# Flow attention: inverses as 128 columns, spread by plain fp32 matmuls one chunk at a time

## What is computed

```
q = sigmoid(q); k = sigmoid(k)
sink_incoming    = 1 / sum_d((q + EPS) * (k.sum(n) + EPS))
source_outgoing  = 1 / sum_d((k + EPS) * (q.sum(n) + EPS))
conserved_sink   = sum_d((q + EPS) * ((k * source_outgoing).sum(n) + EPS)) + EPS
conserved_source = clip(sum_d((k + EPS) * ((q * sink_incoming).sum(n) + EPS)) + EPS, -1, 1)
v    = v * softmax_n(conserved_source) * n
kv   = k^T v                                     # 32 x 32 in each head
out  = (q * sink_incoming) kv * sigmoid(conserved_sink)
out  = out @ proj_w.T + proj_b
```

## Time and profile before

| | |
|---|---|
| time, median of 3 runs | 2605.04 us (2602.89 to 2608.36) |
| profiled execution: its own time | 2608.17 us |
| its span on the core | 2606.3 us |
| mean granted clock of TensorE | 0.979 |
| TensorE busy | 2350.9 us, 90% of the span |
| VectorE busy | 1591.2 us, 61% |
| ScalarE busy | 1247.5 us, 48% |
| GpSimd busy | 691.7 us, 27% |

### The profile page before, as it was taken

One profiled execution on the slowest core, in us unless ns is written; L12 is line 12 of the kernel. 1 busy time (PEld: TensorE's weight loads), 2 busy tenths in 40 slices (PEclk: granted clock), 3 DMA queues, 4 the chain that ended last, 5 costly groups with the idle time before them and its releaser, 6 DMA issues.

```text
span 2606.3 us, 37060 instructions
## 1 busy us (share of the span) xinstructions
PE 2350.9 (90%) x13000; PEld 1303.8 (50%) x13000; DVE 1591.2 (61%) x3101; ACT 1247.5 (48%) x2870; POOL 691.7 (27%) x989
## 2 busy tenths in 40 slices
PE   7989999989988999998898999999899899999866
PEld 3655544545565544454556554435455655444443
DVE  4664643569866462457977655155797746516698
ACT  5763212259675321227967431222886723122396
POOL 0002140037401232013820213201480031310366
PEclk9999999999999999999999999999999999999988
DMA  8001010010210200001030101001003010100000
GB/s 300 18 11 49 24 45 33 0 49 1 87 50 10 72 29 17 32 1 49 9 128 2 55 26 29 32 17 49 1 9 128 2 58 23 29 17 1 0 1 33
DMA packets 58988, 99.43 MB, mean 38 GB/s; under 512 B 13364, under 2 KB 13748, under 8 KB 58296
## 3 DMA queue, kind: packets, MB, share of 16 engines
q1 hardware_dynamic: 58808, 97.06, 11.3%
HBM read 88.66 MB, written 8.39 MB: 37 GB/s over the span
## 4 chain that ended last, share of the span: by engine, by line
PE 61%; DVE 18%; ACT 14%; issue 4%; POOL 2%; DMA 0%; ACTq 0%; DVEq 0%; POOLq 0%; SPq 0%
PE psum L398 20%; PE psum L392 13%; ACT prob L810 6%; PE psum L424 4%; PE psum L483 3%; DVE neg_max L1106 3%; PE psum L549 2%; DVE f_a L1113 2%; PE psum L451 2%; PE psum L791 2%; DVE bn L1056 2%; DVE f_top L1392 2%; PE psum L620 1%; ACT f_z L1008 1%; PE psum L763 1%
## 5 line engine op out<-in xcount | busy, mean ns | idle before, releaser
L398 PE MATMUL psum<-weights,mixed 128*128 128x512 f32 x768 | 341.2, 595 | 0.0
L392 PE MATMUL psum<-xT,weights 128*128 128x512 f32 x768 | 334.5, 593 | 0.0
L810 ACT ACTIVATE prob<-psum,neg_max 128x128 f32<-128x128 f32 (+3 forms) x512 | 265.0, 543 | 109.3 <-DVE neg_max L1106 109.3
L1430 POOL TENSOR_SCALAR var<-stats 128x1 f32<-128x1 f32 x192 | 63.8, 332 | 797.2 <-DVE stats L1057 797.1
L1106 DVE TENSOR_REDUCE neg_max<-psum 128x1 f32<-128x128 f32 (+3 forms) x512 | 217.5, 483 | 81.2 <-PE psum L488 46.5
L846 ACT COPY xT<-psum 128x512 f32<-128x512 f32 x128 | 70.3, 590 | 367.4 <-PE psum L451 367.4
L1087 DVE TENSOR_TENSOR x<-psum,x 128x512 f32<-128x512 f32 x128 | 88.4, 691 | 244.8 <-PE psum L398 172.7
L398 PE MATMUL psum<-weights,xT 128*128 128x512 f32 x512 | 232.9, 598 | 2.4 <-DVE recip L1295 1.6
L1443 POOL TENSOR_TENSOR f_a<-f_a,f_z 128x256 f32<-128x256 f32 x256 | 204.5, 809 | 113.8 <-DVE f_a L1113 113.8
L392 PEld LDWEIGHTS psum<-xT,weights 128*128 128x128 f32 x768 | 144.0, 190 | 172.4 <-issue 172.2
L398 PEld LDWEIGHTS psum<-weights,mixed 128*128 128x128 f32 x768 | 141.6, 190 | 167.5 <-issue 166.7
(11 more groups left out here) (246 smaller groups left out, 4193.1 us busy)
## 6 DMA issues: line engine op xcount, KB each, us to landing
xT<-in_xT SPq DMA_DIRECT2D x8, 1024.0 KB, 6.4
x<-in_x SPq DMA_DIRECT2D x8, 1024.0 KB, 8.9
out<-x SPq DMA_DIRECT2D x16, 512.0 KB, 2.8
weights<-in_a_k SPq DMA_DIRECT2D x4, 1024.0 KB, 5.3
weights<-in_a_q SPq DMA_DIRECT2D x4, 1024.0 KB, 5.1
weights<-in_a_v SPq DMA_DIRECT2D x4, 1024.0 KB, 5.0
w1f<-in_w SPq DMA_DIRECT2D x4, 1024.0 KB, 14.9
w2f<-in_w SPq DMA_DIRECT2D x4, 1024.0 KB, 17.3
```

The lines of the kernel that those rows point to most:

```text
L392: last = mm(bank[:, 0:n], weights[weight][:, c, heads(g)], rhs(c), start=(c == 0), stop=(c == C - 1))
L398: last = mm(bank, lhsT(c), weights[weight][:, c, :], start=(c == 0), stop=(stop and c == C - 1))
L810: last = run(sb["prob"][:, slot, o:o + keys], bank[:, o:o + keys], ACT.Exp, bias=sb["neg_max"][:, n, qc, j:j + 1], accum_out=sb["a_sum"][: ...
```

## The change

The inverses are held as 128 columns instead of 512: a quarter (tile) c of a window is laid on partitions 2c and 2c + 1 of each head's eight. For that a total is computed by 16 matmuls of 128 columns (`d_quarters`: four quarters of four chunks, accumulated) with `d_thin` widened to four quarters. The split in coarse half and remainder is gone from ScalarE and GpSimd; each spread bank is filled by four plain fp32 matmuls of 32 rows (those of the chunk), 128 stationary columns (`d_sel`) and 128 moving columns (`d_inv`), chunk after chunk. The two source sums go to one bank (256 columns), with one exponential and one transpose of 128x128 for each window. Each of the four constants has its own `d_weights` and `d_sums`; the one for the q sums, a total and a spread move in among the last projections of k. `d_project` is a step for each chunk. In this stage `dve_ring` has banks 6 and 7 as well. The core of the diff (left out: declarations of tiles, semaphores and constants, and the same steps in other words):

```diff
+    def widen(self, banks):
+
+        n = len(self.names)
+        k = (n - self.first) % len(self.banks)
+        self.banks, self.first = banks + self.banks[k:] + self.banks[:k], n
+
+    def narrow(self, pe, banks):
+
+        self.drained(pe)
+        self.banks = banks
...
-              ("weight", 12), ("transpose", 3, 4), ("d_project", 0, 0), ("transpose", 3, 5), ("transpose", 3, 6), ("transpose", 3, 7),
-              ("d_project", 0, 1), ("bias", 3, 0), ("bias", 3, 1), ("d_project", 1, 0), ("d_project", 1, 1)]
+              ("weight", 12), ("transpose", 3, 4)]
+    steps += [("d_project", 0, 0, g) for g in range(C)] + [("transpose", 3, 5), ("transpose", 3, 6), ("transpose", 3, 7)]
+    steps += [("d_project", 0, 1, g) for g in range(C)] + [("bias", 3, 0), ("bias", 3, 1)] + [("d_project", 1, 0, g) for g in range(C)]
+    steps += [("d_weights", OF_Q), ("d_project", 1, 1, 0), ("d_sums", OF_Q), ("d_total", 1), ("d_project", 1, 1, 1), ("d_project", 1, 1, 2),
+              ("d_spread", 1), ("d_project", 1, 1, 3), ("d_table",)]
     if b < B - 1:
         steps += [("weight_ahead", 1), ("weight_ahead", 2)]
-    steps += [("d_sums",), ("d_total", 0), ("d_turn", 0), ("d_total", 1), ("d_turn", 1), ("d_value", 0), ("d_turn", 2), ("d_value", 1),
-              ("d_spread", 0), ("d_total", 2), ("d_value", 2), ("d_turn", 3), ("d_spread", 1), ("d_total", 3), ("d_value", 3), ("d_turn", 4),
-              ("d_value", 4), ("d_spread", 2), ("d_value", 5), ("d_turn", 5), ("d_value", 6), ("d_spread", 3), ("d_value", 7), ("d_turn", 6),
-              ("d_turn", 7), ("d_sums2",), ("d_source", 0), ("d_source", 1), ("d_sink", 0, 0), ("d_sink", 0, 1), ("d_weigh", 0), ("d_weigh", 1), ("d_sink", 0, 2), ("d_sink", 0, 3), ("d_kv",)]
+    steps += [("d_turn", 0), ("d_turn", 1), ("d_total", 3), ("d_weights", OF_K), ("d_value", 0), ("d_sums", OF_K), ("d_total", 0), ("d_spread", 3),
+              ("d_value", 1), ("d_total", 2), ("d_spread", 0), ("d_weights", OF_SINK), ("d_value", 2), ("d_turn", 2), ("d_spread", 2),
+              ("d_value", 3), ("d_sums", OF_SINK), ("d_weights", OF_SOURCE), ("d_value", 4), ("d_turn", 3),
+              ("d_sums", OF_SOURCE), ("d_source",), ("d_value", 5), ("d_turn", 4), ("d_turn", 5), ("d_value", 6), ("d_weigh", 0), ("d_turn", 6),
+              ("d_turn", 7), ("d_value", 7), ("d_weigh", 1)] + [("d_sink", 0, g) for g in range(C)] + [("d_kv",)]
...
+            def d_quarters(bank, i, src, w):
+
+                for c in range(WT):
+                    for g in range(C):
+                        last = mm(bank[HD * g:HD * g + HD, :], sb["d_thin"][:, i, c, g, :], src[:, g, w * D + P * c:w * D + P * c + P],
+                                  start=(c == 0), stop=(c == WT - 1))
+                return last
...
                 elif kind == "d_value":
...
                 elif kind == "d_sums":
 
-                    pe.wait_ge(q["d_weights_ready"], at("d_weights_ready", 2))
+                    i, = arg
+                    if i == SUM_ORDER[0]:
+                        dve_ring.widen([banks[6], banks[7]])
+                    pe.wait_ge(q["d_weights_ready"], at("d_weights_ready", SUM_ORDER.index(i) + 1))
                     bank = dve_ring.claim(pe, step)
-                    for i in range(2):
+                    if i == OF_SINK:
+                        last = mm(bank[:, 0:C], sb["blocks"][:], sb["d_tot"][:, i, :], start=True, stop=True)
+                    else:
...
+                            last = mm(bank[HD * g:HD * g + HD, 0:C], thin_blocks, sb["d_tot"][:, i, :], start=True, stop=True)
...
                 elif kind == "d_total":
                     w, i = divmod(arg[0], 2)
-                    d_compact(dve_ring.claim(pe, step), i, sb[("d_qT", "d_kT")[i]], w)
+                    taken(pe, (("d_q", "d_k")[i], w, C - 1))
+                    d_quarters(dve_ring.claim(pe, step)[:, 0:P], i, sb[("d_qT", "d_kT")[i]], w).then_inc(dve_ring.filled, 1)
...
                 elif kind == "d_spread":
 
                     n, = arg
-                    pe.wait_ge(q["d_halves_ready"], at("d_halves_ready", n + 2))
+                    pe.wait_ge(q["d_inverse_ready"], at("d_inverse_ready", TOTAL_ORDER.index(n) + 1))
                     for g in range(C):
-                        mm(dve_ring.claim(pe, ("d_spread", n, g)), sb["d_sel_r"][:, g, :], sb["d_halves"][:, n % 2, :],
-                           start=True, stop=True).then_inc(dve_ring.filled, 1)
-                elif kind == "d_sums2":
-                    pe.wait_ge(q["d_weights_ready"], at("d_weights_ready", 4))
+                        r = slice(HD * g, HD * g + HD)
+                        bank = dve_ring.claim(pe, ("d_spread", n, g))
+                        for c in range(WT):
+                            last = mm(bank[:, heads(c)], sb["d_sel"][r, c, :], sb["d_inv"][r, n, :], start=True, stop=True)
+                        last.then_inc(dve_ring.filled, 1)
+                elif kind == "d_source":
                     bank = dve_ring.claim(pe, step)
-                    for g in range(C):
-                        mm(bank[HD * g:HD * g + HD, 8:10], sb["d_thin"][:, 2, g, :], sb["flow_eps"][:], start=True, stop=True)
-                    for g in range(C):
-                        last = mm(bank[:, 2 * g:2 * g + 2], sb["d_blk"][:, C + g, :], sb["flow_eps"][:], start=True, stop=True)
+                    for w in range(W):
+                        last = d_quarters(bank[:, heads(w)], OF_SOURCE, sb["d_kT"], w)
                     last.then_inc(dve_ring.filled, 1)
-                elif kind == "d_source":
-                    d_compact(dve_ring.claim(pe, step), 2, sb["d_kT"], arg[0])
...
-                    pe.wait_ge(q["d_e_ready"], at("d_e_ready", w + 1))
-                    bank = dve_ring.claim(pe, step)
-                    for t in range(WT):
-                        last = nc.tensor.transpose(bank[:, heads(t)], sb["d_inv"][:, W + w, heads(t)], ident[:])
-                    last.then_inc(dve_ring.filled, 1)
+                    pe.wait_ge(q["d_e_ready"], at("d_e_ready", 1))
...
+                    pe.wait_ge(q["d_shares_ready"], at("d_shares_ready", 1))
+                    mm(dve_ring.claim(pe, ("d_esum",))[:, 0:C], sb["d_sel"][:, WT, :], sb["d_shares"][:], start=True, stop=True)\
+                        .then_inc(dve_ring.filled, 1)
...
                 elif kind == "d_sink":
                     w, g = arg
+                    pe.wait_ge(q["d_weights_ready"], at("d_weights_ready", SUM_ORDER.index(OF_SINK) + 1))
...
+                    if w + t == 0:
+                        dve_ring.narrow(pe, banks[3:6])
...
+                elif kind == "d_table":
                     load_table(1, ACT.Exp)
-                    copy(sb["d_sel_r"][:], sb["d_sel"][:]).then_inc(q["d_halves_ready"], 1)
-                elif kind == "d_total":
-                    n, = arg
-                    act.wait_ge(q["d_inverse_ready"], at("d_inverse_ready", n + 1))
-                    if n >= 2:
-                        written(act, ("d_spread", n - 2, C - 1))
-                        act.wait_ge(q["d_halves_ready"], at("d_halves_ready", n))
-                    run(sb["d_coarse"][:, n % 2, :], sb["d_inv"][:, n, :], ACT.Copy, scale=sb["odd_rows"][:]).then_inc(q["d_coarse_ready"], 1)
...
                 elif kind == "d_source":
-                    w, = arg
-                    act.wait_ge(q["d_logits_ready"], at("d_logits_ready", w + 1))
-                    run(sb["d_inv"][:, W + w, :], sb["d_inv"][:, w, :], ACT.Exp,
-                        accum_out=sb["d_esum"][:, w:w + 1]).then_inc(q["d_e_ready"], 1)
+                    act.wait_ge(q["d_logits_ready"], at("d_logits_ready", 1))
+                    run(sb["d_e"][:], sb["d_log"][:], ACT.Exp, accum_out=sb["d_esum"][:]).then_inc(q["d_e_ready"], 1)
...
-            def eps_weights(sums, out, blocks):
-
-                link(v.scalar_tensor_tensor(sb["d_tot"][:], sums[:, 0, :], FLOW_EPS, sums[:, 1, :], ALU.add, ALU.add))
-                v.tensor_tensor(out, blocks, sb["d_tot"][:, :, None].broadcast_to([P, *out.shape[1:]]), ALU.mult)\
-                    .then_inc(q["d_weights_ready"], 1)
+            def eps_weights(i, sums, out, pattern):
+
+                of_chunk = sb["d_tot"][:, i, :]
+                link(v.scalar_tensor_tensor(of_chunk, sums[:, 0, :], FLOW_EPS, sums[:, 1, :], ALU.add, ALU.add))
+                each = of_chunk[:, :, None].broadcast_to([P, C, P]) if i == OF_SINK else \
+                    of_chunk[:, None, :, None].broadcast_to([P, WT, C, HD])
+                v.tensor_tensor(out, pattern, each, ALU.mult).then_inc(q["d_weights_ready"], 1)
...
+            quarters = sb["quarters"][:][:, :, None, :].broadcast_to([P, WT, C, HD])
...
+                elif kind == "d_weights":
+                    i, = arg
+                    if i in (OF_Q, OF_K):
+                        taken(dve, (("d_k", "d_q")[i], 1, C - 1))
```

(59 more changed lines are left out.)

87 lines of the change are left out of this document (28 added, 59 removed).

## The result

The changed kernel takes 2588.81 us (median of 4 runs, 2585.42 to 2590.64), the kernel before, run beside it, 2606.35 us (2602.89 to 2608.36): ratio 0.9933, 95% interval 0.9915 to 0.9950. It is faster, by 17.5 us. The forecast was 2593.6 us in a range of 2584 to 2607.

A forecast was written before the change was run, and what follows sets the result against it. TensorE bounds the kernel, except where a stage makes it wait. 2.5 us a batch, 10.0 in four, plus 1.4 in the first make 11.4 us off the 2605.04 median: 2593.6 us, range 2584 to 2607.

The forecast's parts named there:

- The sign and the main mechanism: Flow attention: faster, as 6.8 us of TensorE waits (0.5 stay) and 1.7 us of clock come back per batch.
- second slow piece: First batch's two source sums, 3.58 us there and 1.92 in the model batch; its going gives 1.4 us more.
- the spreads' border term: Spreads: a bank's first record may start beside the previous bank's last; at most 1.3 us a batch saved, 0.6 taken.
- the 0.2 us for entering and leaving: Spreads: entering and leaving the 32-row shape costs 0.2 us for each of four groups, 0.8 us a batch.
- The 0.48 us sink wait: TensorE's wait for a bank before the last of four sinks, 0.48 us, assumed to stay.
- the forecast's stretch: From the projections to the first output row block: 98.5 us a batch, against 27.44 + 73.59 = 101.0.
- Behind the output block's start nothing changes, so what the stage gains reaches the end: After flow attention: the gain, 2.5 us a batch plus 1.4 in the first, 11.4 us, shows whole in the kernel time.
- 1: Rival, spreads: weight loads not hidden on a repeated row set, 0.21 us a record, kernel 2642 us; chance 0.09.
- 2: Rival, spreads: quarter-row work drops the clock to half for 3.4 us at each spread, kernel 2621 us; chance 0.08.
- 3: Rival, new TensorE-VectorE hand-overs: 2 us a batch of unseen waits left, kernel 2601.6 us; chance 0.15.
- 4: Rival, spreads: neighbouring banks overlap more, all borders free and no entry cost, 13.2 us, kernel 2588 us; chance 0.13.
- the small sums, transposes and records of exponentials: Flow attention on TensorE: the small sums, transposes and records of exponentials save 2 us a batch.

The follow-up runs named there:

- e2: Changed kernel with every spread matmul reading rows 0 to 31 (chunk 0's inverses), so the row set never changes and part of the computation differs: 2618.05 us.
- e3: Changed kernel with every spread matmul reading all 128 rows, so each bank gets the sum over four chunks: 2597.91 us.
- e5: Changed kernel with spreads filled two chunks at a time, 0 and 1 alternating, then 2 and 3: 2565.08 us against 2607.73.
- e1: Changed kernel with all four spread banks claimed first and a quarter of each chunk in turn, each matmul on another 32-row set: 2559.14 us, ratio 0.9819.
- e4: Changed kernel with each spread bank written twice by the same four matmuls, 64 records a spread instead of 32, same result: 2701.08 us.
- e6: Changed kernel with the ring kept at three banks in this stage, without banks 6 and 7: 2597.30 us.
- e7: Changed kernel with q sums, first total and first spread behind all key projections, two key turns between total and spread: 2590.20 us.
- e8: Changed kernel with an unused 128x512 reciprocal (3.35 us) on VectorE ahead of each real one: 2614.10 us.
- e10: The changed kernel again, unaltered, 5 rounds: 2587.67 us against 2606.42, ratio 0.9926, span 2585.9 us.

## Why the prediction was right, and where its size was off

**The sign and the main mechanism** held. The waits for VectorE and the stretch at half clock went, the clock is 1.00 in all batches, and the first batch won 1.4 us more than the others (7.2 against 5.8), as its second slow piece said.

**The step that was mis-sized is the spreads' border term**: "the first record of a bank may start beside the last one of the bank before", at most 0.11 us a border, of which half was taken. Measured, three records of one bank run beside three of the other: 0.34 us a border. Four spreads are 11.0 us, against 14.7 with a floor of 13.2. The rate inside a bank (0.113 forecast, 0.112 measured) and the 0.2 us for entering and leaving were right; e2 and e3 show them apart, e5 and e1 that the rule carries to other orders.

**The other terms.** Reciprocals took 0.953 us (0.95), the totals 1.0 each (1.01). The 0.48 us sink wait, kept in the forecast, is gone. What wasn't counted: a wide group right behind a step of 32 rows or 32 columns takes 3.54 to 3.63 us instead of 3.44 (1064.07 to 1067.61, 1069.65 to 1073.28), about 1.0 us a batch. So the forecast's stretch, from the start of `d_project` (1, 0), is 95.3 us (109.08 less the 13.8 in front), not 98.5: -3.7 - 0.5 + 1.0 = -3.2.

**"Behind the output block's start nothing changes, so what the stage gains reaches the end"** failed in part. Its instructions are the same, but two batches had a long half-clock stretch there: 2 x 0.96 + 2.05 + 1.83 = 5.8 us, by the longer windows in the first and third batch; another 0.6 is a later start of the very first scores, and the stretches from scores to stage, -1.4 to +1.4 us each, nearly cancel. Together: 11.4 forecast, + 13.2 in the stages (24.6 against 11.4), - 6.5 = 18.1, which is the span's difference. The two errors go against each other, so that 2588.8 lies only 4.8 us from the forecast is in part luck: the stages alone gave more than twice what was forecast for them.

**The rivals.** 1 is false: e2 has the repeated row set, the 187 ns loads and 112 ns between starts, where 0.21 us was its price. The Trainium skill, in TensorE: Matmul & The Clock Gate, under "What overlaps and what doesn't", gives the rule behind it, a weight load overlaps only if its row group differs; the trace disagrees. 2 didn't happen in the change but does when one row set works alone (e2) or spreads are twice as long (e4). 3 is false: no wait is left in the stage, and e6 to e8 show that single losses of cover cost 0.3 to 5.3 us a batch. 4 names the right direction, and its 2588 is the time measured, but not for its reason: its floor of one record a border was itself passed, by 0.55 us a spread.

**What of this is only argued.** That the number of records in sequence on a row set sets the time is shown in four arrangements (the change, e1, e2, e5). Why three records of the next bank get ahead, and not one or eight, isn't. That the length of the half-clock stretch behind the stage goes with where a batch falls in time fits e10, but nothing was run that moves a batch without changing it. That the small sums, transposes and records of exponentials that went save some 2 us a batch was worked out from rows of before; no run takes them by themselves. Why the clock fell behind some spreads of e2 and not behind others is open too.

**The better version** is e1: 2559.14 us, 46.7 us or 1.8% under the kernel before and 28.5 under e10, with the same records, banks and waits as the change. Its stages give 26.3 of the 27.4 us between its span and e10's; e10's 57.03 and 138.16 us behind the second stage are 56.08 and 136.27 in it.

## What to carry to other kernels

When matmuls use only 32 rows, let each follow one on another row set: count the records in sequence on each set, not the records. A hand-over that looks free in a walk is free only with the rest of the cover; take covers away together, too, before calling one of them unnecessary. And a stage's gain is to be read in the stage: what the whole kernel shows also holds what the clock did behind it.

## What the hardware showed that was not expected

- 32 fp32 records of 32x128 by 128 columns took 3.77 us on one row set, 2.75 chunk after chunk, 1.65 in pairs, 1.10 with four sets in turn: a factor of 3.4 between one row set and four in turn, and 2.5 of order alone (2.75 against 1.10). The Trainium skill, in TensorE: Matmul & The Clock Gate, under "Measured speedup vs the span model", gives 3.07 for four row tiles with 512 moving columns. This case's 3.4, with fp32 and 128 columns, is of that size.
- At a border between two row sets, with eight records or more on each, three records of the next set start beside the last three of the one before; a border saves 0.34 us.
- Right behind a spread of 3.77 us on one row set (two of the four in the first batch), with no pause on TensorE, the granted clock fell to the 1.2 GHz level; it was there for most of the next 3.41 us (0.61 in the mean); behind 2.75 us over four sets in turn, and behind 3.57 us on all rows, it stayed at 1.00.
- Entering and leaving the 32-row shape costs 0.2 us a spread (e2 against e3, 3.77 and 3.57 us), and the first wide record behind it another 0.10 us (eight take 3.54 us instead of 3.44).
- The same instructions behind the stage took 3.0 us longer in a batch whose half-clock stretch was 13.7 us than in one with 6.8.
